# The first eight quads' rows made in setup, and a looser wait of GpSimd

## The reference

```python
h_s = s @ lin1_ws * a * _inv(S_IN)
h_v = jnp.einsum('nci,cd->ndi', v, lin1_wv) * a[:, :, None] * _inv(V_IN)
hid = jax.nn.silu(edge_scalars @ fc_w1 * _inv(R))
w = hid @ fc_w2 * _inv(FC_HID)
es, ev = h_s[edge_src], h_v[edge_src]
...
agg_s = jax.ops.segment_sum(mid_s, edge_dst, num_segments=n) * inv_nn
agg_v = jax.ops.segment_sum(mid_v, edge_dst, num_segments=n) * inv_nn
...
x = _layernorm(x + concatenate([scalars, gated]))
```

## Time and profile before

| what | value |
|---|---|
| time, median of 3 runs | 4014.98 us |
| span of the profiled execution | 4805.3 us |
| granted TensorE clock, mean | 0.952 |
| busy: TensorE matmul, weight load | 3953.4 us, 1603.5 us |
| busy: VectorE, ScalarE, GpSimd | 2421.9 us, 1987.8 us, 2967.8 us |
| gathers on GpSimd | 3125, mean 945 ns each |
| first edge gather, last edge gather | 74.72 us, 4767.37 us |

### The profile page before, as it was taken

One profiled execution on the slowest core, in us unless ns is written; L12 is line 12 of the kernel. 1 busy time (PEld: TensorE's weight loads), 2 busy tenths in 40 slices (PEclk: granted clock), 3 DMA queues, 4 the chain that ended last, 5 costly groups with the idle time before them and its releaser, 6 DMA issues.

```text
span 4805.3 us, 64016 instructions
## 1 busy us (share of the span) xinstructions
PE 3953.4 (82%) x18658; PEld 1603.5 (33%) x18658; DVE 2421.9 (50%) x7622; ACT 1987.8 (41%) x5178; POOL 2967.8 (62%) x3160
## 2 busy tenths in 40 slices
PE   8778888888888888888888888888888888888887
PEld 5233333333333333333333333333333333333333
DVE  5455545555454544555555445555545545454544
ACT  3344444444444444344444344444444434444444
POOL 3666666666666666666666666666666666666664
PEclk9999999999999999999999989999999999999999
DMA  6443434343434343334343334343434333333333
GB/s 216 146 106 102 106 102 106 102 107 102 108 99 108 102 106 97 105 102 106 103 107 101 104 99 105 102 106 103 107 103 106 102 105 103 105 103 104 103 103 87
DMA packets 366207, 515.47 MB, mean 107 GB/s; under 512 B 66498, under 2 KB 245578, under 8 KB 365486
## 3 DMA queue, kind: packets, MB, share of 16 engines
q0 software_dynamic: 150768, 256.60, 22.7%
q10 hardware_dynamic: 164378, 180.74, 12.1%
q1 hardware_dynamic: 50724, 74.13, 5.1%
HBM read 431.15 MB, written 80.06 MB: 106 GB/s over the span
## 4 chain that ended last, share of the span: by engine, by line
another core or an unknown queue 35%; ACT 21%; PE 20%; issue 14%; ACTq 8%; SPq 0%; DMA 0%; DVE 0%; DVEq 0%
ACT aggsb L759 13%; ACTq L778 6%; PE pst_e L1061 6%; PE psg L1074 5%; PE psg L1072 5%; ACT tsum L783 3%; PE psw L1053 3%; ACTq L766 2%; ACT L804 1%; ACT hid L749 1%; PE psx L1097 1%; PE psx L1045 1%; ACT vec_s L800 0%; ACT L749 0%
## 5 line engine op out<-in xcount | busy, mean ns | idle before, releaser
L710 POOL DMA_INDIRECT rows<-h_table,src_cols x3125 | 2953.5, 945 | 1799.9 <-issue 894.8
L557 DVE TENSOR_TENSOR prod<-psw,rows 128x384 f32<-128x384 f32 (+2 forms) x3128 | 1210.1, 449 | 1680.8 <-remote 1264.3
L1072 PE MATMUL psg<-tsum,shifts 128*64 128x320 f32 x3126 | 1101.8, 478 | 653.3 <-ACT tsum L783 462.6
L1053 PE MATMUL psw<-fc,hid 128*128 128x448 f32 x3128 | 1424.0, 579 | 7.7 <-issue 1.7
L759 ACT ACTIVATE aggsb<-psg 32x160 f32<-32x160 f32 x3128 | 917.0, 293 | 927.2 <-remote 744.2
L1074 PE MATMUL psg<-tsum,shifts 128*64 128x288 f32 x3126 | 1009.2, 449 | 0.0
L1053 PEld LDWEIGHTS psw<-fc,hid 128*128 128x128 f32 x3128 | 549.0, 196 | 949.6 <-issue 840.1
L1061 PE MATMUL pst_e<-prod,sel 128*32 128x448 f32 x6256 | 811.9, 593 | 2.4 <-issue 2.4
L1072 PEld LDWEIGHTS psg<-tsum,shifts 128*64 128x64 f32 x3126 | 385.9, 144 | 1122.2 <-ACT tsum L783 774.3
L783 ACT ACTIVATE tsum<-pst_e 128x448 f32<-128x448 f32 x782 | 424.8, 543 | 499.0 <-remote 369.4
L1045 PE MATMUL psx<-es,fc 128*128 128x512 f32 x782 | 415.7, 613 | 175.5 <-ACT turned L788 120.5
(11 more groups left out here) (151 smaller groups left out, 1511.2 us busy)
## 6 DMA issues: line engine op xcount, KB each, us to landing
es<-in_esP ACTq DMA_DIRECT2D x391, 256.0 KB
agg_table<-aggsb ACTq DMA_DIRECT2D x782, 80.0 KB
rows<-h_table,src_cols POOLq DMA_INDIRECT x3125
nag<-agg_table SPq DMA_DIRECT2D x96, 320.0 KB
nxin<-in_xN SPq DMA_DIRECT2D x96, 208.0 KB
h_table<-hrow ACTq DMA_DIRECT2D x24, 320.0 KB, 4.2
out<-yn SPq DMA_DIRECT2D x95, 80.0 KB
xa<-in_xaT SPq DMA_DIRECT2D x24, 256.0 KB, 4.0
```

The source lines that it names most:

```text
L557: return nc.vector.tensor_tensor(out, w_part, ev, ALU.mult)
L710: nc.gpsimd.indirect_dma_start(out=rows[:, u * QT + j, :], out_offset=None, in_=m.h, in_offset=bass.IndirectOffsetOnAxis(ap=m.src[:, t:t + ...
L1053: ins = nc.tensor.matmul(psw[b][:, 2 * c:2 * c + 2, 0:WN], hid[:, at:at + P], m.fc2[:].rearrange("p (t w) -> p t w", t=2)[:, :, 0:WN], sta ...
L1072: nc.tensor.matmul(psg[0:2 * W, 0:2 * AW].rearrange("p (s c) -> p s c", s=2), shifts[:, q % PRING, h, 0:2, :], low, start=(h == 0), stop=( ...
```

## The change

The block of setup gets eight more units among its 25 chunks. The list `UNITS` holds both kinds in the order in which every engine takes them: `("h", c)` is a chunk as before, `("x", j)` makes the scaled rows of quad `j`, straight into `rows`. After chunks 6, 9, 11, 14, 16, 19, 21 and 24 comes one of them. GpSimd gathers the x rows with their node attribute (input `xg`, 161 floats a row) by the source nodes of the first 32 tiles; TensorE turns four tiles (`turn`), one unit ahead; ScalarE and VectorE copy what is turned; TensorE then runs the same linear layer on it. In every unit ScalarE now scales the first half and VectorE the second. VectorE's checks are cut into pieces, one piece ahead of the copy of each unit; the offsets use a new input with the first node of each quad in place of eight narrow operations, and the widest check goes over 780 values, not 3124. The buffers of x and `h` lie inside the edge attributes' array, whose later part is loaded only after the stores of `h` have landed; the last weight loads move from GpSimd's to SyncE's queue. The wait for the stores of `h` moves from SyncE at the end of setup to GpSimd in the edge block, and VectorE's products of the first eight quads wait for no gather.

In the edge block GpSimd starts with quad 8, and `freed` sets its waits: quads 8 to 15 each wait for the quad that had the slot (`q - 8`), later pairs for the two quads that had their two slots.

```diff
+AHEAD = RING
+XBEFORE = [6, 9, 11, 14, 16, 19, 21, 24]
+UNITS = [unit for c in range(HCHUNKS + 1) for unit in [("h", c)] + [("x", j) for j in range(AHEAD) if XBEFORE[j] == c]]
...
-            for c in range(1, SLOTS):
-                load_x(c, c, CB * P)
+            for c in range(1, 4):
+                load_x(c, CB * P)
             sp.dma_start(m.dst[:], io["dstT"]).then_inc(s_dst, 16)
             sp.dma_start(tbase[:], io["tile_base"].to_broadcast([P, TILES])).then_inc(s_dst, 16)
...
+            for c in range(4, HCHUNKS):
+                load_x(c, CB * P)
...
-            for c in range(SLOTS):
-                sp.wait_ge(s_hout[c], 16 * (rounds + (2 if c == 0 else 0)))
...
+            pool.wait_ge(s_src, 16)
+            for t in range(AHEAD * QT):
+                nc.gpsimd.indirect_dma_start(
+                    out=xg[:, t, :], out_offset=None, in_=io["xg"],
+                    in_offset=bass.IndirectOffsetOnAxis(ap=m.src[:, t:t + 1], axis=0)).then_inc(s_xrow[t // QT], 16)
...
+                if n + 1 < len(UNITS) and UNITS[n + 1][0] == "x":
+                    j = UNITS[n + 1][1]
+                    dve.wait_ge(s_xrow[j], 16 * QT)
+                    nc.vector.tensor_copy(xlast[:].rearrange("p (t c) -> p t c", c=V),
+                                          xg[:, QT * j:QT * j + QT, P:F]).then_inc(s_xlast, 1)
+                if kind == "x":
+                    dve.wait_ge(s_xps, c + 1)
+                    nc.vector.tensor_copy(xzt[:], pxz[:, 0:P]).then_inc(s_xzcp, 1)
...
+                high_half(n, kind, c)
...
+            def turn(j):
+
+                pe.wait_ge(s_xrow[j], 16 * QT)
+                for t in range(QT):
+                    nc.tensor.matmul(pxt[:, P * t:P * t + P], xg[:, QT * j + t, 0:P], m.ident[:], start=True, stop=True,
+                                     is_transpose=True, skip_group_check=True)
+                pe.wait_ge(s_xlast, j + 1)
+                nc.tensor.matmul(pxz[:, 0:P], xlast[:], m.ident[:], start=True, stop=True,
+                                 is_transpose=True, skip_group_check=True).then_inc(s_xps, 1)
...
+                else:
+                    pe.wait_ge(s_xcp, c + 1)
+                    pe.wait_ge(s_xzcp, c + 1)
+                    left, last = xt[:], xzt[:]
...
+            for n, (kind, c) in enumerate(UNITS):
+                if kind == "x":
+                    act.wait_ge(s_xps, c + 1)
+                    nc.scalar.activation(xt[:], pxt[:], ACT.Copy).then_inc(s_xcp, 1)
+                low_half(n, kind, c)
+                if n and UNITS[n - 1][0] == "h":
+                    store(UNITS[n - 1][1])
...
+            for c in range(len(m.h_stored)):
+                pool.wait_ge(m.h_stored[c], m.h_stores[c])
+                pool.sem_inc(stores_seen, 1)
...
+            def freed(q):
+
+                if q < 2 * RING:
+                    return q - RING + 1
+                if q % GROUP:
+                    return 0
+                return q - RING + GROUP
+
             with pool.If(miss == 0):
-                for q in range(QUADS):
+                for q in range(AHEAD, QUADS):
                     for j in range(QT if q < QUADS - 1 else LAST_REAL):
-                        gather(q, j, max(0, q - 2) if j == 0 and q % GROUP == 0 and q >= GROUP else 0)
+                        gather(q, j, freed(q) if j == 0 else 0)
...
-                dve.wait_ge(rows_loaded[u], 16 * (QT * I + tiles))
+                if loaded:
+                    dve.wait_ge(rows_loaded[u], 16 * (QT * (I - 1) + tiles))
```

More of the change, by code:

```diff
@@ L55 @@
 CB = 4
+SLOTS = 8
 AGG_ROWS = 99 * P
@@ L180, in setup_block @@
         s_xin = [sem(f"x_loaded{c}") for c in range(SLOTS)]
[L181 to L188, removed]
+        s_xrow = [sem(f"x_rows_loaded{j}") for j in range(AHEAD)]
+        s_xlast = sem("x_last_joined")
+        s_xps = sem("x_turned_in_psum")
+        s_xcp = sem("x_turned_copied")
+        s_xzcp = sem("x_last_copied")
+        s_low = sem("low_half_in_psum")
+        s_high = sem("high_half_in_psum")
+        s_lowcp = sem("low_half_copied")
+        s_highcp = sem("high_half_copied")
+        s_tick = sem("setup_ticks")
+        s_hout = m.h_stored
+        rest = N - HCHUNKS * CB * P
+        done = CB * HCHUNKS
         block = ctx.enter_context(nc.Block())
@@ L205, in setup_block @@
             late.append((m.fc1[r, r], io["fc_w1"]))
-        n_w = 16 * (len(loads) + len(late))
+        n_w, n_fcw = 16 * len(loads), 16 * len(late)
         @block.sync
@@ L239, in _ @@
+            for c in range(4, HCHUNKS):
+                load_x(c, CB * P)
+            load_x(HCHUNKS, rest)
+            sp.dma_start(m.e4[:, 0:E4_FIRST, :], io["e4T"][:, 0:E4_FIRST, :]).then_inc(s_edge, 16)
+            sp.wait_ge(s_fc, 1)
+            sp.sem_inc(s_tick, 1)
+            for dst, src in late:
+                sp.dma_start(dst, src).then_inc(s_fcw, 16)
+            sp.wait_ge(s_edge, 16)
+            sp.wait_ge(s_fcw, n_fcw)
             sp.wait_ge(m.es_loaded, 16)
@@ L281, in _ @@
             last.then_inc(s_lw, 1)
[L282 to L299, removed]
@@ L305, in axis @@
             def axis(t, r, i):
                 return t[r, :].rearrange("p (d i) -> p d i", i=3)[:, :, i]
[L308 to L314, removed]
-                else:
-                    last = nc.vector.tensor_scalar(axis(chunk[:, SO:2 * SO], r, to), l2v[r, part, :], scale, None, ALU.mult)
@@ L392, in _, with half @@
-            for c in range(SLOTS):
-                chunk(c, 0, [P] * CB, 32, c >= 2)
-                if c == 0:
+            def half(n, v, widths, left, last):
+                for b in range(2):
+                    out = psh[n % 2][0:widths[b], v, F * b:F * b + P]
+                    nc.tensor.matmul(out, left[:, (2 * v + b) * P:(2 * v + b) * P + widths[b]], lw1[:], start=True, stop=True)
+                r = slice(S * v, S * v + S)
+                both = psh[n % 2][:, v, 0:2 * F].rearrange("p (b f) -> p b f", f=F)[:, :, P:F]
+                return nc.tensor.matmul(both, last[r, :], lw1z[r, :], start=True, stop=True)
@@ L395, in _ @@
                     pe.wait_ge(s_row, 1)
-                    for n in range(2):
-                        ins = nc.tensor.matmul(psp[:, n:n + 1], rowp[:, n, :], ones[0:1, 0:1], start=True, stop=True)
+                    for k in range(2):
+                        ins = nc.tensor.matmul(psp[:, k:k + 1], rowp[:, k, :], ones[0:1, 0:1], start=True, stop=True)
                     ins.then_inc(s_place, 1)
-            with pe.Fori(1, rounds) as i:
-                for c in range(SLOTS):
-                    chunk(c, i, [P] * CB, 32 * (i + 1), True)
@@ L963, in round_of @@
                 for u in range(quads):
-                    products(R, u, LAST_REAL if quads < RING and u == quads - 1 else QT)
+                    products(R, u, not first, LAST_REAL if quads < RING and u == quads - 1 else QT)
                     if finishing and u == 2:
```

341 lines of the change are left out of this document (227 added, 114 removed).

## The result

The changed kernel takes 4078.18 us (median of 4 runs, 4073.3 to 4086.85) against 4014.96 us of the kernel before on the same chip (4014.46 to 4015.94): a ratio of 1.0159, with a 95% interval of 1.0145 to 1.0174. It is 63 us slower. I had forecast slower by 26 us, with 4064 as the upper end. The way was right; the forecast size was less than half of what came.

A forecast was written before the change was run, and what follows sets the result against it. The prediction took GpSimd's back-to-back gathers, after a setup bound by TensorE, to bound the kernel. Added setup work and waits less 40.0 us of gathers summed to +25.8, from 4015 to 4041 us, range 3998 to 4064.

The forecast's parts named there:

- 32 gathers fewer: Edge block: GpSimd no longer gathers the first 32 tiles after setup, 1.25 us each, -40.0 us.
- matmuls and transposes at the full clock: Setup on TensorE: eight new units add matmuls, +15.2 us, and five transposes each, +8.0 us.
- waits for ScalarE and VectorE in the units: New units in setup: TensorE waits for ScalarE's copies, +7 us, and VectorE's joins and copies behind its checks, +19 us.
- chunk 4 behind dst and tbase: Setup, SyncE's queue: chunk 4's x lands later than TensorE wants it, +4 us (0 to 8).
- TensorE's clock: Setup: waits above 3 us lower the granted clock, up to 4.4 us an occasion, +5 us (0 to 17).
- end of setup: Between setup's last matmul and edge work: no wait for the last h rows to land, -2.3 us (0 to -3).
- first gather waits for quad 0's sum: Start of edge block: GpSimd's gather for quad 8 waits until quad 0 is summed and frees the slots, +9.9 us.
- looser wait: GpSimd's pair waits in the edge block: loosening them gains 0, as plain runs hardly pause.
- the cover holds: Rival, setup: VectorE's and ScalarE's links and chunk 4 are hidden, clock stays; 4008 to 4016 us, chance 0.15.
- The looser wait pays: Rival, edge block: GpSimd waits for late sums at pairs in plain runs too; 4003 down to 3850 us, chance 0.17.
- each wait costs its pause: Rival, edge block: GpSimd's waits cost about 1.95 us each in plain runs too; 4052 us, chance 0.07.
- TensorE paces the plain runs: Rival, edge block: TensorE, not GpSimd, sets the pace, so fewer gathers give nothing; 4069 us, chance 0.07.

The follow-up runs named there:

- the run with both edits: Changed kernel with chunks 4 to 7 of x loaded ahead of dst and tbase, and VectorE's joins and copies ahead of its checks: 4045.82 us, ratio 1.0073.
- with the links hidden: Changed kernel with old load order, join and copies one unit earlier, checks two units later, keep-warm ahead of new units: 4007.72 us, ratio 0.9984 to the kernel before.
- the run without the keep-warm: Changed kernel with old load order, join and copies one unit earlier, checks two units later, no keep-warm ahead of new units: 4016.41 us, ratio 0.9981 to the kernel before.

## Why the prediction was right in its way and wrong in its size

Taken by the steps of the prediction, between the profiled executions (the sum 173.71 - 74.72 = 99.0 us for the first edge gather):

| step | forecast | measured |
|---|---|---|
| 32 gathers fewer | -40.0 | -40.0: 3092 x 1.250 remain |
| matmuls and transposes at the full clock | +15.2 + 8.0 | taken as forecast; see below |
| waits for ScalarE and VectorE in the units | +7 + 19 | +22.1, thirteen gaps |
| chunk 4 behind dst and tbase | +4 (0 to 8) | +8.4 |
| TensorE's clock | +5 (0 to 17) | +38.8, the rest of 92.5 |
| end of setup | -2.3 | 1.90 - 4.39 = -2.5 |
| first gather waits for quad 0's sum | +9.9 | 9.57 - 0.58 = +9.0 |
| looser wait | 0 | 0 by itself; the tight one would cost 15.1 once |

The measured terms add up to +59.0, and the profiled run took 4073.3 us, 58 above the kernel before. (The 32.7 us behind the last gather run to the end of the span, which is 1.8 us shorter than the run; the forecast's 34 runs to the run's end, so the two agree.) The median lies 5 us higher still; the spread of setup told above would make that, but those runs have no profile.

Late in setup, at the full clock, a new unit took 1.97 us and its transposes 0.95 (140.99 to 142.96, 145.53 to 146.48); eight of both are 23.4, near the 23.2 of the forecast. The matmuls of setup ended at 162.24 in place of 69.76, 92.5 us later. Less 23.2, 22.1 and 8.4 that leaves 38.8 for the clock. The other way, by rows: 16 chunks, from chunk 4 to 19, lie between 28 and 139 us, nearly all at the low level, at 4.38 - 2.44 = 1.94 us each, 31 at most; five new units and their transposes there add some 2 us each, 10: 41 at most, near it.

**The step that failed** is "TensorE's clock ... Four of the waits above exceed 3 us; an occasion costs up to 4.4 us of matmul time". It priced an occasion by the earlier trace rows, the end of setup, where the records show the clock back after 10 us. There TensorE came back from its wait to the edge block's matmuls. In setup it came back to chunks with a new wait every second or third one, and the clock stayed at 0.50 for 58 and then 55 us. So the price was not an occasion's but that of nearly all matmuls in the stretch: 38.8 us, where the forecast had 5. Why the level stays low so long is open, since 13.4 us without a wait (46.11 to 59.51) didn't end it. I also took waits under 3 us to be harmless; the run with both edits has 0.50 with gaps of 0.83. The clock term's upper bound of 17 came from the same thought, so the range was too narrow. (Chunk 4's wait, 8.4, also lay just above its bound of 8.)

The rest of the working held: the sum without the clock and chunk 4 came within 5 us, and the waits on VectorE stand where they were forecast (the 4.15 us is the copy behind the 3.40 us reduction before the second new unit). Without the clock's 38.8 the measured terms still give +20, so that the way of the forecast was not luck. That the pauses of the profile were not in the plain runs, inferred from three numbers, is shown by the second profile of the kernel before: a wait already met costs nothing there, as no wait of GpSimd between gathers takes over the usual 0.3 us. The sentence from the Trainium skill that I weighed there, GPSIMD Engine Reference, section Instruction dispatch, doesn't say this: it speaks of one Pool instruction's completion and the next Pool instruction, not of a wait for TensorE, and the step from it was mine. My forecast that as many pauses would be in the profile after was wrong for the same reason.

Of the rivals, "the cover holds" named the right remedy: with the links hidden the time was 4007.72, its lower end of 4008. That the number fits so well is in part luck, as that kernel also has eight keep-warms more, some 4 us. "The looser wait pays" and "each wait costs its pause" are out by the run with the looser wait alone (4014.68) and by the second profile of the kernel before. "TensorE paces the plain runs" is out: 3092 gathers at 1.250.

## What to carry to other kernels

Where TensorE runs in lockstep with copies on other engines, price a new wait by its clock too: take as the upper bound what all matmuls from there to the end of the disturbed stretch lose at half speed, not the length of the gap. Have what the next step on TensorE needs copied a step earlier, ahead of long off-path work on the same engine; where a gap can't be avoided, matmuls on constants in it can pay for themselves, as they did here. And have a surprising profile taken a second time before a term is built on it, when its span and the plain time disagree.

## What was not expected of the hardware

TensorE busy for 9.45 of 10 us (110 to 120 us of the changed kernel) still ran at a granted clock of 0.50, and 9.20 of 10 with a single gap of 0.83 us did as well. Yet over the whole execution TensorE is busy for 93% with many gaps, and the mean granted clock of the changed kernel is 0.979, setup included. The shape of setup's matmuls is not enough to explain it: with next to no waits the same ones had 1.00 (20 to 60 us of the run without the keep-warm). What makes the difference wasn't tried.

Adding 36 us of matmuls made a kernel 26 us faster. And one profiled execution of the kernel before held 788 us of GpSimd pauses that no other profiled execution showed.
